# Five or four PSUM banks for the y products of a DLRM tower with a compressed interaction network, on one Trainium2 core

## The reference

```python
def _cin_layer(xi, x0, W, b):
    Fi, F0 = (xi.shape[1], x0.shape[1])
    Wr = W.reshape(Fi, F0, -1)
    out = jnp.einsum('nie,nje,ijo->noe', xi, x0, Wr) + b[None, :, None]
    return jax.nn.relu(out)
x0 = inputs
xs = [x0]
for W, b in ((W1, b1), (W2, b2), (W3, b3)):
    xs.append(_cin_layer(xs[-1], x0, W, b))
z = jnp.concatenate(xs, axis=1).sum(axis=-1)
h = jnp.concatenate([z, dense_ctx], axis=1)
h = jnp.maximum(h @ W_top1 + b_top1, 0.0)
h = jnp.maximum(h @ W_top2 + b_top2, 0.0)
y = h @ W_top3
```

## Time and profile before

| what | us |
|---|---|
| median of 3 runs | 2390.68 (2388.43 to 2391.88) |
| profiled execution, its own time | 2390.02 |
| its span | 2388.1 |
| PE busy | 2307.3 (97%) |
| DVE busy | 2214.5 (93%) |
| ACT busy | 2133.4 (89%) |
| POOL busy | 1971.2 (83%) |

### The profile page before, as it was taken

The page is one execution under the profiler, slowest core; times in us unless marked ns, Lnnn a source line. Parts: engine busy times, 40 slices in busy tenths (PEclk is TensorE's granted clock), DMA queues, the critical chain, the costliest instruction groups (busy, mean ns, idle before and its releaser), DMA issues.

```text
span 2388.1 us, 67815 instructions
## 1 busy us (share of the span) xinstructions
PE 2307.3 (97%) x14174; PEld 1191.7 (50%) x14174; DVE 2214.5 (93%) x8839; ACT 2133.4 (89%) x7973; POOL 1971.2 (83%) x2254
## 2 busy tenths in 40 slices
PE   1699999999999999999999999999999999999999
PEld 0355555555555555555555555555555555555553
DVE  6499999999999999999999999999999999999995
ACT  4589999999999999999999999999999999999995
POOL 7589888888888888888888888888777777777774
PEclk6799999999999999999999999999999999999999
DMA  5133333333333333333333333333333333333331
GB/s 174 29 73 68 70 72 73 66 69 73 71 65 71 72 72 64 72 73 69 67 72 72 71 66 72 72 69 66 72 70 65 68 70 70 63 71 72 68 68 36
DMA packets 150185, 168.19 MB, mean 70 GB/s; under 512 B 111940, under 2 KB 115655, under 8 KB 150120
## 3 DMA queue, kind: packets, MB, share of 16 engines
q0 software_dynamic: 42864, 136.87, 31.1%
q1 hardware_dynamic: 107256, 30.73, 5.7%
HBM read 12.82 MB, written 0.00 MB: 5 GB/s over the span
## 4 chain that ended last, share of the span: by engine, by line
PE 88%; issue 4%; ACT 3%; POOL 2%; DMA 1%; SPq 1%; DVE 1%; ACTq 0%; DVEq 0%; POOLq 0%
PE y L521 76%; PE m L511 8%; PE m L493 3%; ACT work L635 2%; DMA work<-work 1%; POOL zl L396 1%; DVE acc L858 1%; POOL part L361 0%; ACT work L665 0%; ACT zh L663 0%; PE y L546 0%; PE y L599 0%; SPq L257 0%; POOL part L363 0%; POOL emb L301 0%
## 5 line engine op out<-in xcount | busy, mean ns | idle before, releaser
L521 PE MATMUL y<-whi,xT 128*128 128x512 f16 x6144 | 1990.0, 379 | 5.1 <-DMA xT<-lo 3.9
L635 ACT ACTIVATE work<-y,xc 128x128 f32<-128x128 f32 x5632 | 1615.4, 430 | 132.1 <-PE y L521 95.7
L858 DVE SCALAR_TENSOR_TENSOR acc<-y,xc,acc 128x128 f32<-128x128 f32 x5632 | 1616.4, 341 | 72.0 <-PE y L521 65.3
L521 PE MATMUL y<-wlo,xT 128*128 128x512 f16 x3072 | 1164.8, 379 | 0.0
L521 PEld LDWEIGHTS y<-whi,xT 128*128 128x128 f16 x6144 | 599.2, 98 | 624.1 <-ACT work L635 12.5
L521 PEld LDWEIGHTS y<-wlo,xT 128*128 128x128 f16 x3072 | 300.8, 98 | 237.0
L361 POOL TENSOR_TENSOR part<-work 128x512 f32<-128x512 f32 x255 | 324.2, 1271 | 83.3 <-DMA work<-work 61.4
L396 POOL TENSOR_TENSOR zl<-work,zh 128x1152 f16<-128x1152 f32 x128 | 343.3, 2682 | 7.2 <-ACT work L665 7.2
L334 POOL DMA_DIRECT2D work<-work x255 | 229.1, 899 | 103.3 <-ACT work L635 102.4
L301 POOL DMA_INDIRECT emb<-tbl,ids_sb x192 | 201.4, 1049 | 47.0 <-issue 44.2
L665 ACT ACTIVATE work<-m 128x512 f32<-128x512 f32 (+1 forms) x384 | 224.2, 584 | 0.0
(11 more groups left out here) (109 smaller groups left out, 2082.1 us busy)
## 6 DMA issues: line engine op xcount, KB each, us to landing
work<-work POOLq DMA_DIRECT2D x255, 512.0 KB, 4.8
xT<-hi SPq DMA_TRANSPOSE x256, 4.5
xT<-lo SPq DMA_TRANSPOSE x256, 3.4
emb<-tbl,ids_sb POOLq DMA_INDIRECT x192, 2.5
xx<-w SPq DMA_DIRECT2D x4, 768.0 KB
work<-w SPq DMA_DIRECT2D x4, 768.0 KB
x0T<-x0hl SPq DMA_TRANSPOSE x128
wt_sb<-W_top SPq DMA_DIRECT2D x1, 768.0 KB
```

The costliest lines, as they stand in the source:

```text
L521: ins = nc.tensor.matmul(dst[:], xT[layer][:, parity, a, :], w[layer][:, cols], start=i == 0, stop=i == 2)
L635: nc.scalar.activation(prods[layer][:, a, k * P:(k + 1) * P], bank[:, k * P:(k + 1) * P], ACT.Copy, scale=xc[layer][:, parity, j:j + 1]).t ...
L858: ins = nc.vector.scalar_tensor_tensor(dst, y, col, mine, ALU.mult, ALU.add)
```

## The change

The ring gets four banks. The fifth becomes `misc[2]`, and group 1 of the pair sums is put there. Group 1 then waits for the squares of its own group of the tile before (`s_zts` at 3t - 1), and the wait for the pooling of the tile before goes to the start of layer 1, which writes `misc[0]`. In the dense tower `misc[2]` takes the place of `ybank[4]`.

```diff
-RING = 5
+RING = 4
...
-PAIR_BANK = (1, 0, 1)
+PAIR_BANK = (1, 2, 1)
...
-        misc = [ps(f"m{n}", [P, Q * P]) for n in range(2)]
+        misc = [ps(f"m{n}", [P, Q * P]) for n in range(3)]
...
-        h1bank = [misc[0], misc[1], ybank[4], ybank[0]]
+        h1bank = [misc[0], misc[1], misc[2], ybank[0]]
...
                 elif g == 1:
-                    wait(pe, s_pool[0], t + 1)
+                    wait(pe, s_zts, t * 3 - 1)
...
                 if c == 0:
                     wait(pe, s_zts, t * 3 + 3)
+                    wait(pe, s_pool[0], t + 1)
```

## The result

The changed kernel takes **2444.76 us** (median of 3 runs, 2444.59 to 2445.32) where the kernel before took 2390.68: a ratio of 1.0225, with a 95% interval of 1.0211 to 1.0239. That is 54.1 us more. The forecast was 2453 us in a range of 2430 to 2470. The profiled execution took 2445.32 us, its span is 2443.5 us, 55.4 us more than that of before.

What follows compares the result with a forecast made beforehand. PE was taken as the bound; stalls at item 16 of 39.1 us (odd), 13.6 (even) and 9.1 (late even steps), with restarts and a handover gain of 1.3 each, gave +62 us: 2453 us, range 2430 to 2470.

Steps and rivals of the forecast that it cites:

- What bounds it: PE is the bound in the steady stretch, busy 1078.91 and 1078.57 of 1080 us, with no idle time to make up stalls.
- The freed wait and the new waits: Group 1's dropped wait for pooling: 0, at most 3.0 us gained; added waits on the tile before: 0.
- The place and price of the stall: PE's item 16 waits for DVE's item 12: 0.62 us in odd steps, 0.31 in even, 0.48 in even from 90 on.
- The handover and the restart: 0.05 us from an evacuation's end to PE's next matmul, and 0.01 us more before the second matmul.
- The largest demand counts, the others don't add: Within a step only item 16's 0.62 us is paid; item 23's 0.57 us on ACT's item 19 falls within it.
- The closed loop: Rival: consumers go late with PE, so stalls at items 16 and 23 add; 114 us, about 2505 us, chance 0.06.
- the term of the late even steps: Stall at item 16 in the 19 even steps from 90 on, 0.48 us each, 9.1 us in all.
- its upper bound: 2470 us, if all steps paid the odd price, as when DVE's long small instruction came in other even steps too.
- What the profile after would show: Weight loads waiting for DVE at item 16, steps of 18.3 us (odd) and 18.0 (even), the clock full.
- two signs: PE busy near 1048 of 1080 us, and its y weight loads waiting for DVE some 126 times.
- The clock: Rival: PE's clock falls to 1.2 GHz in one step in ten, 220 us, about 2675 us; chance 0.01.

Runs made afterwards that it cites:

- the ring of four alone: Changed kernel with group 1's pair sums back in their old two banks and their old wait for the pooling, four banks kept: 2443.29 us, ratio 1.0231.
- all waits but that one: Kernel before, five banks, PE made to wait for item n-4 before every item n from 4 on except item 16: 2429.80 us, ratio 1.0168.
- DVE's chain shortened: Changed kernel with DVE's merge and pooling of layer 3 moved from item 11 to item 16, behind item 12: 2426.33 us, ratio 1.0158.

## Why the prediction was right, and where its size was off

*What bounds it.* Right: PE had nothing to make the stall up with, so 54 us of time came out of some 57 us of stalls.

*The freed wait and the new waits.* Taken at 0, and the ring of four alone shows nothing else, within some 5 us. The rule of the Trainium skill (Perfetto Trace Analysis, section Matmuls) that independent groups go through banks of their own brought no gain that can be told here; the shared bank was hardly waited for, 3.0 us in all.

*The place and price of the stall.* Right in both: item 16 on item 12, 0.31 and 0.61 us in the trace for 0.31 and 0.62, and shown by the one wait in the kernel with five banks, which costs the same as the change. Why the odd steps pay more was not read: 0.26 us of it arise up to DVE's wait for ACT's high half. The handover and the restart are those of the earlier trace rows.

*The largest demand counts, the others don't add.* Right: 41 us for all waits but that one, 38 us with DVE's chain shortened, where the sum worked out at 42 for both. The closed loop would have added 114 us for the whole change, where 54 were measured, and in step 61 of the changed kernel items 18, 19 and 23 follow their neighbours at 0.65 us as before. That rules it out.

*The terms that were too large.* The sum was +62 us, 8 us over what was measured. The largest error is the term of the late even steps, 19 x 0.48 = 9.1 us. It took a duration of the trace before that depends on what POOL does beside it. In the changed kernel ACT begins item 19 of step 61 at 1226.58, 4.37 us after PE's middle matmul of item 15, and before it was 4.35 us after it, though PE has been held by 0.61 us in between. So ACT, and POOL, which waits for ACT's items, are earlier against PE and DVE, and the small instruction loses little time. That POOL is earlier is in the rows of steps 94 and 96 above; the link from ACT to POOL fits them, but no run took it apart. Line 827 takes 0.37 us in the late steps (6.72 / 18) and DVE passes none of it on: in step 94 items 15 and 16 are 0.97 us apart, the stall of an early even step. From step 110 on, the even stalls are 0.21 us: items 15 and 16 of step 112 are 2150.10 - 2149.23 = 0.87 us apart. The views for both, line 827 by stretches and PE's timeline:

```profile
1690.00:2340.00 650.00, 6.72 (x18) 1.00 0.36 67
...
1822.49 0.38 PE L522 MATMUL y<-wlo,xT 128*128 128x512 f16 x1
...
1823.46 0.38 PE L522 MATMUL y<-wlo,xT 128*128 128x512 f16 x1
...
2149.23 0.38 PE L522 MATMUL y<-wlo,xT 128*128 128x512 f16 x1
...
2150.10 0.38 PE L522 MATMUL y<-wlo,xT 128*128 128x512 f16 x1
```

With 0.31 us for the ten even steps to 108 and 0.21 for the rest the term is about 5 us, so it was 4 us too large. The prediction has a shift of POOL against DVE only behind its upper bound, as something that would make stalls longer; here it made them shorter. A smaller part is the late odd steps: from step 109 on the stall is 0.14 us shorter than the 0.62 of step 61 that the sum uses for all of them, 1 us too many.

The remaining 3 us are of two kinds. Added up over both traces, the distances between neighbouring y items grow by 57.9 us at item 16 and shrink by 2.7 us at all others together, which are short waits that PE had before in some steps and no longer has (1.8 us of them at item 1 of the even steps). The sum took 1.3 us for them, 1.4 too few. The other 1.2 us are the choice of runs: the two profiled executions are 55.3 us apart, the medians 54.1.

*What the profile after would show.* The place was right, and so were the steps: 1223.48 - 1205.18 = 18.30 us for the odd one, and 18.00 us to the same matmul of step 62 (1241.48). But two signs were read wrongly. PE's busy time is 1062 of 1080 us and not 1048, since the drawn-out matmuls cover 0.16 us of each stall, and the waits of the weight loads are 418 and not 126, as they wait beside running matmuls too. The distance between the starts of the matmuls is the measure: it needs no end of a matmul and no releaser.

*The clock.* It stayed at its full level, 2.4 GHz, in every slice from the third on, with 127 stalls of 0.2 to 0.6 us. The Trainium skill (TensorE: Matmul & The Clock Gate, section A second HAM failure mode: psum-queue depth-cycling) tells of a kernel that went through its PSUM banks with short idle times and whose clock went up and down for it. This trace doesn't agree: the granted clock is 1.00 in both stretches. No run here shows what the difference is.

## What to carry to other kernels

Before taking a buffer from a ring, go through one period of the trace, subtract the end of each item's consumer from the start of the item that would reuse its buffer, and take the largest lack of the period, not the sum: in this kernel that was the price per period, since the producer is the bound and the consumers meet it again in each period. Then look at what stands between the consumer's last wait for the producer and that item; here 1.7 us of small work (0.75 + 0.60 + 0.35), moved away from between them, gave back some 50 of the 54 us that the buffer was worth. A duration that depends on a neighbour engine (a small VectorE instruction beside a GpSimd one) isn't a constant to multiply with.

## What wasn't expected of the hardware

A VectorE instruction on 2 elements per partition took 0.83 us in place of 0.16 to 0.2 in the kernel before, when a GpSimd tensor_tensor had begun 0.25 us before it; it ended 0.04 us after that one, and so it did in the changed kernel, where it started later and took 0.20 us. Beside a GpSimd indirect DMA that had begun before, it took 0.30 us and ended at 1310.74, 0.04 us after the 1310.70 at which that one ended. But it isn't held by the whole of such an instruction: in step 62 of the changed kernel it starts at 1231.91, 0.27 us after one that runs from 1231.64 for 1.07 us, and takes 0.16 us.

```profile
1231.64 1.07 POOL L301 DMA_INDIRECT emb<-tbl,ids_sb  x1 [0.17 <-issue]
...
1231.91 0.16 DVE L827 TENSOR_SCALAR mx<-mx 128x2 f32<-128x2 f32 x1
```
